# A graph layer's edge loop: the tiles that hold gathered table rows go from a ring of 6 to a ring of 12, placed in space that the unsorted records have left

## The chip, the cores and the metric

The kernel is one program on one core of a Trainium2 chip. Its time is the device time of one execution in microseconds (us). The kernel before was timed three times; the median counts. A separate profiled execution left the trace.

## The reference, cut to what matters

The layer has 1250 nodes of 512 features and 41250 edges, and then a feed-forward part with eight experts. Only the graph part touches the change:

```
xs = x[:, :C] @ W_in2f_s ; xv = einsum(x[:, C:], W_in2f_v)     # one table row of 4*128 values per node
sj = xs[idx_j] ; vj = xv[idx_j]                                # GATHER: one table row per edge
h  = shifted_softplus(f_ij @ Wf1 + bf1)                        # 20 radial values per edge -> 128
W  = (h @ Wf2 + bf2) * rcut_ij                                 # filter of each edge
s2, v2 = products of sj, vj and the edge's direction, times W
agg = segment_sum(x_ij, idx_i)                                 # sum over the edges of each target node
```

(Of the six parts of `W` the kernel needs four, since the last two feed nothing in the output.)

## The kernel before, in words

A first stage normalizes the nodes, builds the table `table_d` (1250 rows of 512 float32) in HBM, sorts the edges into 20 buckets by target node, and writes the edges' records back to HBM as `rec_d`. The unsorted records sit in the on-chip region `region_u` (10336 float32 per partition) until that write is over; after the edge loop the same region takes the transposed sums and then weights of the experts.

The edge loop (about 200 to 1256 us) goes through 342 tiles of 128 edges. Four tiles are a quad; three quads are one body of the hardware loop (12 tiles). What each engine does for tile t:

- GpSimd (POOL) issues two indirect DMAs, in one in-order queue. `gather_record(t + 6)` (L552) fetches 128 records of 32 values; it first waits until the product of the tile twelve before that record's tile is done (`prod_ready`), and its one-hots too. `gather_source(t)` (L563) fetches 128 table rows of 512 values by the indices in the record; it waits for the quad's records and, from t = 6 on, for `s_done`, the end of the summing matmuls of tile t - 6. Its target is `gath[:, t % 6]`. The POOL program is written out for all tiles, so its waits are on constants.
- TensorE (PE): per quad four `second_layer` matmuls (L1077, the filter W into a PSUM bank, ends `w_ready`), after the third of them `first_layer` of the next quad (L1068, ends `m1_done`), then four `sum_tile` (L1089 and L1096, which add the products into a bank by one-hots, end `s_done`). `sum_tile(t)` waits for `prod_ready` and for `flushed` of tile t - 3.
- VectorE (DVE): `products(t)` is two multiplications, L906 and L908; before them it waits for the rows (`rows_in`) and for `w_ready`. Between products stand `flush` (L920, adds a bank to the sums; one of a ring of three banks), `one_hot` (L897), `hidden` (L883) and `transpose_records` (L889, needs the records two quads ahead). In each quad the order is: product 0, flush of the quad before's tile 3, one-hot, products 1 to 3, flush 0, one-hot, hidden, flush 1, one-hot, transpose, flush 2, one-hot.
- ScalarE (ACT): scaled one-hots, the softplus (L669 waits for `m1_done`), and `seed`, which puts the constant part of W into a bank.
- SyncE's queue loads the residual input and the weights of one expert during the loop, each load after a given `prod_ready`.

After the loop come the node stage and the experts, which the change does not touch.

Of the kernel before, what the change touches and what calls it, by code (L numbers as in the profile page):

```python
# [15 lines left out]
P = 128  # L16
NODES, HID, FDIM, EDGES, RBF = 1250, 512, 128, 41250, 20
# [14 lines left out]
QUAD = 4  # L32
USED = (EDGES + BUCKETS * (P - 1)) // P
# [35 lines left out]
def tiles_of(left):  # L69

    return QUAD if left >= 1 else LAST
# [4 lines left out]


RING = 3
GRING = 6
PRING = 4  # L80
SRING = 3
SUM_BANKS = (0, 1, 7)
# [48 lines left out]
def hold(eng, semaphore, value, passed):  # L131

    eng.wait_ge(semaphore, value)
    eng.sem_inc(passed, 1)  # L134


def build(nc, x, src, rec_in, w_s, w_v, wf1, bf1, wf2, bf2, w1s, w1v, w2s, w2v,
          wg, wu, bu, wd, bd, out):
    ctx = ExitStack()
    with ctx:  # L140
        def sb(name, shape, dtype=F32):
            return ctx.enter_context(nc.sbuf_tensor(name, shape, dtype))

        def sem(name):
            return ctx.enter_context(nc.semaphore(name))


        table_d = nc.dram_tensor("table_d", [NODES, HID], F32, kind="Internal").ap()
# [4 lines left out]
        region_u = sb("region_u", [P, NCOLS * REC])  # L153
# [22 lines left out]
        slot_oh = region_r[:, at_slots:at_far].bitcast(BF16).rearrange("p (g s) -> p g s", g=OH_RING)  # L176
        far = region_r[:, at_far:at_far + FAR * P // 2].bitcast(BF16).rearrange("p (g s) -> p g s", g=FAR)

        gath = sb("gath", [P, GRING, HID])
        prod = sb("prod", [P, PRING, PRODS, FDIM])  # L180
        squares = prod[:, 2:4, :, :].rearrange("p a b c -> p (a b c)")[:, 0:4 * NCOLS].rearrange("p (k j) -> p k j", k=4)
        oneh = sb("oneh", [P, PRING, 4, WIDE])
# [75 lines left out]
        pool_passed = sem("pool_passed")  # L258
# [38 lines left out]
        recs_in = [sem(f"recs_in{r}") for r in range(RING)]  # L297
        rows_in = [sem(f"rows_in{g}") for g in range(GRING)]
        rec_t_ready = sem("rec_t_ready")
# [8 lines left out]
        prod_ready = sem("prod_ready")  # L308
        s_done = sem("s_done")
# [99 lines left out]
        with nc.Block() as block:  # L409
# [42 lines left out]
            def _(pool):  # L452
# [93 lines left out]
                def gather_record(t):  # L546

                    q, k = t // QUAD, t % QUAD
                    if q >= RING:
                        hold(pool, prod_ready, t - RING * QUAD + 1, pool_passed)  # L550
                        pool.wait_ge(ohy_ready, t - RING * QUAD + 1)
                    nc.gpsimd.indirect_dma_start(  # L552
                        out=recs[:, q % RING, k, :], out_offset=None, in_=rec_d,
                        in_offset=bass.IndirectOffsetOnAxis(ap=inv_i[:, t:t + 1], axis=0)).then_inc(recs_in[q % RING], 16)

                def gather_source(t):

                    q, k = t // QUAD, t % QUAD
                    if k == 0:
                        hold(pool, recs_in[q % RING], 16 * QUAD * (q // RING) + 16 * tiles_of(QUADS - 1 - q), pool_passed)  # L560
                    if t >= GRING:
                        hold(pool, s_done, 2 * (t - GRING + 1), pool_passed)
                    nc.gpsimd.indirect_dma_start(  # L563
                        out=gath[:, t % GRING, :], out_offset=None, in_=table_d,
                        in_offset=bass.IndirectOffsetOnAxis(
                            ap=recs[:, q % RING, k, R_DST:R_DST + 1].bitcast(I32), axis=0)).then_inc(rows_in[t % GRING], 16)

                pool.wait_ge(s_recd, 32)
                hold(pool, i_ready, 1, pool_passed)
                pool.wait_ge(s_wready, 2)  # L570
                for t in range(GRING):
                    gather_record(t)
                for t in range(USED):
                    if t + GRING < USED:
                        gather_record(t + GRING)
                    gather_source(t)

            @block.scalar
# [145 lines left out]
            def _(dve):  # L724
# [173 lines left out]
                                            rec[:, R_W:R_W + 1], ALU.is_equal, ALU.mult).then_inc(oh_ready, 1)  # L898

                def products(t, r, k, slot, body):  # L900
                    g, turn = (QUAD * r + k) % GRING, (QUAD * r + k) // GRING
                    s, v = gath[:, g, 0:FDIM], gath[:, g, FDIM:].rearrange("p (i f) -> p i f", i=3)
                    w = ps_w[slot].rearrange("p (k f) -> p k f", k=4)
                    dve.wait_ge(rows_in[g], body * 32 + 16 * turn + 16)
                    dve.wait_ge(w_ready, t + 1)
                    nc.vector.tensor_tensor(prod[:, slot, P_A:P_Q + 1:P_Q - P_A, :], w[:, W_A:W_Q + 1, :],  # L906
                                            s.unsqueeze(1).to_broadcast([P, 2, FDIM]), ALU.mult)
                    nc.vector.tensor_tensor(  # L908
                        prod[:, slot, :, :].rearrange("p (g k) f -> p g k f", g=2)[:, :, 1:4, :],
                        w[:, W_D:W_B + 1, :].unsqueeze(2).to_broadcast([P, 2, 3, FDIM]),  # L910
                        v.unsqueeze(1).to_broadcast([P, 2, 3, FDIM]), ALU.mult).then_inc(prod_ready, 1)
# [13 lines left out]
                def step(q, r, body, left=RING, first=False):  # L925

                    nxt, nbody, t = (r + 1) % RING, body + (r + 1) // RING, QUAD * q
                    here, then = tiles_of(left), tiles_of(left - 1)
                    products(t, r, 0, 0, body)
                    if not first:  # L930
                        flush_of(q - 1, (r - 1) % RING, 3)
                    if here == QUAD:
                        one_hot(t + 3, r, 3, 3, body, first=first)
                    for k in range(1, here):
                        products(t + k, r, k, k, body)
                    flush_of(q, r, 0, first=first)
                    if left >= 1:
                        one_hot(t + QUAD, nxt, 0, 0, nbody, n=then)
                        hidden(q + 1, nxt)
                    if here < QUAD:  # L940
                        return
                    flush_of(q, r, 1)
                    if left >= 1:
                        one_hot(t + QUAD + 1, nxt, 1, 1, nbody, n=then)
                    if left >= 2:
                        transpose_records((r + 2) % RING, body + (r + 2) // RING, n=tiles_of(left - 2))
                    flush_of(q, r, 2)
                    if left >= 1 and then == QUAD:
                        one_hot(t + QUAD + 2, nxt, 2, 2, nbody)
# [724 lines left out]
```

## Time and profile before

| what | us |
|---|---|
| median of 3 runs (1662.01 to 1665.01) | 1663.13 |
| the profiled execution | 1661.82 |
| its span, first to last instruction | 1660.1 |
| TensorE busy (matmuls) | 1366.3 (82%) |
| VectorE busy | 1068.0 (64%) |
| ScalarE busy | 826.0 (50%) |
| GpSimd busy | 797.8 (48%) |

"Busy" is time in instructions; waiting, branches and semaphore work do not count. In the groups by line, the part behind the bar is the idle time of the engine just ahead of these instructions, and what ended it. "remote" means that the wait ended at a semaphore's update for which the profile names no instruction; "issue" is idle time in which the engine waited for nothing that the profile shows.

### The profile page before, as it was taken

What the parts mean: (1) busy time and instruction counts of PE and PEld (TensorE: products, weight loads), DVE (VectorE), ACT (ScalarE), POOL (GpSimd) and SP (SyncE); (2) the same over time, 40 slices, a digit from 0 to 9 for tenths busy, and PEclk for the clock granted to TensorE, in tenths of its full rate; (3) what the DMA queues carried; (4) which work ended last, traced back from release to release, by engine and by line L of the source; (5) the groups of instructions that cost most, each with busy time, mean ns of one, the idle gap of its engine ahead of it and who ended that gap; (6) DMA issues with size and microseconds to landing.
All of it is one profiled execution on the core that took longest, in us unless ns stands there. A gap on an engine that the chain in (4) does not pass through costs nothing. (4 is left out here: it accounts for less than half of the span.)

```text
span 1660.1 us, 26803 instructions
## 1 busy us (share of the span) xinstructions
PE 1366.3 (82%) x7054; PEld 776.0 (47%) x7054; DVE 1068.0 (64%) x2530; ACT 826.0 (50%) x2145; POOL 797.8 (48%) x844
## 2 busy tenths in 40 slices
PE   0777688888888888888888888888899269999997
PEld 0552344444444444444444444444458146555554
DVE  6899567777777777777777777777787731111110
ACT  3679646556556556565565565565565201111111
POOL 2257556656656656666566566566550012222111
PEclk9999799999999999999999999999999569999999
DMA  5044133334333333333333333333342314554531
GB/s 218 1 191 128 37 88 91 104 99 106 103 86 106 94 96 105 107 104 111 104 100 94 88 88 94 87 91 91 87 106 89 130 57 142 168 179 144 148 81 20
DMA packets 65670, 172.66 MB, mean 104 GB/s; under 512 B 13963, under 2 KB 22523, under 8 KB 64989
## 3 DMA queue, kind: packets, MB, share of 16 engines
q0 software_dynamic: 43424, 105.53, 24.7%
q1 hardware_dynamic: 22196, 66.57, 11.2%
q8 instruction: 18, 0.29, 0.1%
q14 instruction: 32, 0.26, 0.1%
HBM read 148.72 MB, written 18.08 MB: 100 GB/s over the span
## 5 line engine op out<-in xcount | busy, mean ns | idle before, releaser
L1096 PE MATMUL PS<-prod,oneh 128*64 128x256 f32 x2052 | 508.4, 389 | 122.1 <-DVE region_s L920 87.2
L563 POOL DMA_INDIRECT gath<-table_d,recs x342 | 323.1, 945 | 307.1 <-PE PS L1089 211.8
L1096 PEld LDWEIGHTS PS<-prod,oneh 128*64 128x64 f32 x2052 | 259.7, 138 | 362.4 <-DVE prod L908 135.6
L1089 PE MATMUL PS<-prod,oneh 128*64 128x256 f32 x1368 | 375.7, 395 | 28.3 <-issue 26.9
L552 POOL DMA_INDIRECT recs<-rec_d,inv_i x342 | 323.1, 945 | 117.1 <-issue 116.5
L1077 PE MATMUL PS<-wf_sb,h_t 128*128 128x512 f32 x684 | 335.0, 613 | 2.9 <-issue 2.9
L908 DVE TENSOR_TENSOR prod<-PS,gath 128x768 f32<-128x768 f32 x342 | 324.1, 948 | 0.0
L684 ACT ACTIVATE oneh<-oneh,recs 128x64 f32<-128x64 f32 x1026 | 272.7, 336 | 77.6 <-issue 40.1
L906 DVE TENSOR_TENSOR prod<-PS,gath 128x256 f32<-128x256 f32 x342 | 143.8, 421 | 201.3 <-remote 152.5
L920 DVE TENSOR_TENSOR region_s<-region_s,PS 128x512 f32 x342 | 233.4, 683 | 44.3 <-issue 33.7
L669 ACT ACTIVATE soft<-PS,b1col 128x512 f32<-128x512 f32 x86 | 59.1, 687 | 322.0 <-remote 314.1
L691 ACT COPY PS<-c_rep 128x512 f32<-128x512 f32 x338 | 186.0, 581 | 43.2 <-DVE prod L908 22.1
L1089 PEld LDWEIGHTS PS<-prod,oneh 128*64 128x64 f32 x1368 | 155.9, 136 | 44.5 <-issue 40.2
L1077 PEld LDWEIGHTS PS<-wf_sb,h_t 128*128 128x128 f32 x684 | 118.6, 194 | 122.0 <-issue 122.0
L897 DVE TENSOR_SCALAR oneh<-iota_f,recs 128x64 f32<-128x64 f32 x342 | 106.0, 310 | 20.4 <-issue 10.1
L1487 ACT ACTIVATE region_s<-PS,bu_col 128x312 f32<-128x312 f32 x64 | 33.3, 520 | 164.3 <-PE PS L1602 164.3
L1068 PEld LDWEIGHTS PS<-rec_t,wf_sb 128*128 128x128 f32 x688 | 91.1, 193 | 46.6 <-issue 40.8
L1545 DVE TENSOR_TENSOR gath<-PS,region_x 128x512 f32<-128x512 f32 (+2 forms) x24 | 14.5, 603 | 139.1 <-PE PS L1617 115.7
L1452 POOL DMA_INDIRECT out<-gath,idx_add x24 | 40.2, 1677 | 128.9 <-ACT gath L1494 128.9
L1442 POOL DMA_INDIRECT region_x<-xn_d,idx_e x24 | 24.3, 1011 | 160.8 <-DVE idx_e L1519 155.1
L1068 PE MATMUL PS<-rec_t,wf_sb 128*128 128x128 f32 x688 | 91.7, 277 | 5.4 <-DVE rec_t L889 5.4
L1010 PE MATMUL PS<-region_r 128*128 128x344 bf16 x323 | 68.7, 314 | 27.5 <-ACT region_r L607 12.9
(270 smaller groups left out, 1481.8 us busy)
## 6 DMA issues: line engine op xcount, KB each, us to landing
region_r<-wu SPq DMA_DIRECT2D x16, 512.0 KB
region_r<-wd SPq DMA_DIRECT2D x16, 512.0 KB
region_u<-wu SPq DMA_DIRECT2D x16, 512.0 KB, 4.3
region_u<-wd SPq DMA_DIRECT2D x16, 512.0 KB, 5.4
recs<-rec_d,inv_i POOLq DMA_INDIRECT x342
gath<-table_d,recs POOLq DMA_INDIRECT x342
region_u<-rec_in SPq DMA_DIRECT2D x1, 5168.0 KB, 17.4
rec_d<-region_u SPq DMA_DIRECT2D x1, 5168.0 KB
```

What stands on the lines that cost most here:

```text
L552: nc.gpsimd.indirect_dma_start(out=recs[:, q % RING, k, :], out_offset=None, in_=rec_d, in_offset=bass.IndirectOffsetOnAxis(ap=inv_i[:, t: ...
L563: nc.gpsimd.indirect_dma_start(out=gath[:, t % GRING, :], out_offset=None, in_=table_d, in_offset=bass.IndirectOffsetOnAxis(ap=recs[:, q % ...
L684: last = nc.scalar.activation(oneh[:, slot, 1 + i, :], oneh[:, slot, 0, :], ACT.Copy, scale=recs[:, r, k, R_VEC + i:R_VEC + i + 1])
L691: nc.scalar.copy(ps_w[slot], c_rep[:, :]).then_inc(seeded, 1)
L897: nc.vector.tensor_scalar(oneh[:, slot, 0, :], iota_f[:, :], rec[:, R_LOCAL:R_LOCAL + 1], rec[:, R_W:R_W + 1], ALU.is_equal, ALU.mult).the ...
L906: nc.vector.tensor_tensor(prod[:, slot, P_A:P_Q + 1:P_Q - P_A, :], w[:, W_A:W_Q + 1, :], s.unsqueeze(1).to_broadcast([P, 2, FDIM]), ALU.mult)
L908: nc.vector.tensor_tensor(prod[:, slot, :, :].rearrange("p (g k) f -> p g k f", g=2)[:, :, 1:4, :], w[:, W_D:W_B + 1, :].unsqueeze(2).to_b ...
L920: nc.vector.tensor_tensor(block, block, PS[:, bank, :], ALU.add).then_inc(flushed, 1)
L1068: last = nc.tensor.matmul(to, wf1_sb[:, k, :], rec_t[:, r, :], start=k == 0, stop=k == QUAD - 1, skip_group_check=True)
L1077: nc.tensor.matmul(ps_w[slot], h_t[:, r, k * P:(k + 1) * P], wf2_sb[:, :, :].rearrange("p k f -> p (k f)"), start=False, stop=True, skip_g ...
L1089: return nc.tensor.matmul(PS[0:WIDE, bank, half * 2 * FDIM:(half + 1) * 2 * FDIM], oneh[:, slot, 0, :], prod[:, slot, 2 * half:2 * half + ...
L1096: return nc.tensor.matmul(to, oneh[:, slot, 1 + i, :], prod[:, slot, P_Q:P_B + i + 1:1 + i, :], start=i == 0, stop=i == 2, skip_group_chec ...
```

## The change

The ring of gathered rows has 12 tiles instead of 6 and lies at the start of `region_u`; `gath` keeps its 6 tiles for its other uses. Each of the 12 tiles has its own semaphore `rows_in`. A gather of rows waits from t = 12 on for the product of tile t - 12 instead of (from t = 6 on) for the sums of tile t - 6. The distance by which records run ahead of rows stays 6 and has a name of its own, `AHEAD`. In the vector program the tile and the awaited value follow from the place in the body alone.

```diff
-GRING = 6
+GRING = QUAD * RING
+AHEAD = 6
...
-        gath = sb("gath", [P, GRING, HID])
+        gath = sb("gath", [P, 6, HID])
+        rows = region_u[:, 0:GRING * HID].rearrange("p (g h) -> p g h", g=GRING)
...
                     if t >= GRING:
-                        hold(pool, s_done, 2 * (t - GRING + 1), pool_passed)
+                        hold(pool, prod_ready, t - GRING + 1, pool_passed)
                     nc.gpsimd.indirect_dma_start(
-                        out=gath[:, t % GRING, :], out_offset=None, in_=table_d,
+                        out=rows[:, t % GRING, :], out_offset=None, in_=table_d,
...
-                for t in range(GRING):
+                for t in range(AHEAD):
                     gather_record(t)
                 for t in range(USED):
-                    if t + GRING < USED:
-                        gather_record(t + GRING)
+                    if t + AHEAD < USED:
+                        gather_record(t + AHEAD)
                     gather_source(t)
...
-                    g, turn = (QUAD * r + k) % GRING, (QUAD * r + k) // GRING
-                    s, v = gath[:, g, 0:FDIM], gath[:, g, FDIM:].rearrange("p (i f) -> p i f", i=3)
+                    g = QUAD * r + k
+                    s, v = rows[:, g, 0:FDIM], rows[:, g, FDIM:].rearrange("p (i f) -> p i f", i=3)
                     w = ps_w[slot].rearrange("p (k f) -> p k f", k=4)
-                    dve.wait_ge(rows_in[g], body * 32 + 16 * turn + 16)
+                    dve.wait_ge(rows_in[g], 16 * body + 16)
```

## Rows read from the trace of the kernel before

**Rows 1.** The page's busy times: us, share of the span, instructions.

```profile
PE 1366.3 (82%) x7054; PEld 776.0 (47%) x7054; DVE 1068.0 (64%) x2530; ACT 826.0 (50%) x2145; POOL 797.8 (48%) x844
```

**Rows 2.** Groups by line and shape, loop only (204 to 1244 us): count, busy us, mean ns, idle before.

```profile
L1096 PE MATMUL PS<-prod,oneh 128*64 128x256 f32 x2017 | 500.5, 389 | 121.2 <-DVE region_s L920 87.2 <-DVE prod L908 16.3 <-issue 16.2
L563 POOL DMA_INDIRECT gath<-table_d,recs x338 | 319.4, 945 | 305.9 <-PE PS L1089 211.8 <-issue 54.3 <-PE PS L1096 34.4
...
L552 POOL DMA_INDIRECT recs<-rec_d,inv_i x331 | 312.4, 944 | 100.9 <-issue 100.5 <-ACT oneh L684 0.3
...
L906 DVE TENSOR_TENSOR prod<-PS,gath 128x256 f32<-128x256 f32 x335 | 140.9, 421 | 198.4 <-remote 152.5 <-PE PS L1077 38.3 <-issue 7.0
...
L889 DVE STREAM_TRANSPOSE rec_t<-recs 128x128 f32<-128x128 f32 x84 | 25.6, 305 | 0.0
```

**Rows 3.** Longest waits in the loop: us in total, times, longest us.

```profile
ACT soft L669 <- remote: 314.1, 82, 4.5
...
DVE prod L906 <- remote: 152.5, 88, 3.7
...
PE PS L1096 <- DVE region_s L920: 87.2, 83, 3.4
```

**Rows 4.** Windows: busy (count) of PE, PEld, DVE, ACT, POOL; clock; DMA share; GB/s.

```profile
260.00:507.70 247.70, 211.82 (x1119) 114.47 (x1119) 187.40 (x360) 143.55 (x380) 151.06 (x160) 0.99 0.37 100
507.70:755.40 247.70, 211.71 (x1124) 113.27 (x1122) 186.89 (x360) 143.63 (x380) 151.13 (x160) 1.00 0.36 101
755.40:1003.10 247.70, 211.43 (x1120) 113.10 (x1119) 187.26 (x360) 143.61 (x380) 151.05 (x160) 1.00 0.35 96
```

**Rows 5.** Row gathers (L563) begun before 508.5 us.

```profile
190.00:508.50 318.50, 96.39 (x102) 0.97 0.36 98
```

**Rows 6.** Products (L906) begun before 500.0 us.

```profile
190.00:500.00 310.00, 40.42 (x96) 0.96 0.36 97
```

**Rows 7.** Timeline of POOL: start, us, instruction, idle before.

```profile
505.05 0.94 POOL L552 DMA_INDIRECT recs<-rec_d,inv_i  x1 [0.30 <-issue]
508.73 0.94 POOL L563 DMA_INDIRECT gath<-table_d,recs  x1 [2.73 <-PE PS L1089]
```

**Rows 8.** Timeline of DVE from product 96 on, same columns.

```profile
500.40 0.42 DVE L906 TENSOR_TENSOR prod<-PS,gath 128x256 f32<-128x256 f32 x1
500.74 0.95 DVE L908 TENSOR_TENSOR prod<-PS,gath 128x768 f32<-128x768 f32 x1
502.06 0.69 DVE L920 TENSOR_TENSOR region_s<-region_s,PS 128x512 f32 x1 [0.37 <-issue]
503.51 0.32 DVE L897 TENSOR_SCALAR oneh<-iota_f,recs 128x64 f32<-128x64 f32 x1 [0.77 <-issue]
504.83 0.42 DVE L906 TENSOR_TENSOR prod<-PS,gath 128x256 f32<-128x256 f32 x1 [1.00 <-issue]
...
507.83 0.42 DVE L906 TENSOR_TENSOR prod<-PS,gath 128x256 f32<-128x256 f32 x1 [0.52 <-remote]
...
517.35 0.42 DVE L906 TENSOR_TENSOR prod<-PS,gath 128x256 f32<-128x256 f32 x1 [1.25 <-PE PS L1077]
...
520.28 0.42 DVE L906 TENSOR_TENSOR prod<-PS,gath 128x256 f32<-128x256 f32 x1 [1.64 <-remote]
```

**Rows 9.** Start of the loop: the third row gather, on POOL.

```profile
199.25 0.95 POOL L563 DMA_INDIRECT gath<-table_d,recs  x1 [0.30 <-issue]
```

**Rows 10.** Start of the loop: the third product, on DVE.

```profile
202.92 0.41 DVE L906 TENSOR_TENSOR prod<-PS,gath 128x256 f32<-128x256 f32 x1
```

**Rows 11.** Line L563: duration ns least/median/most, first and last start us.

```profile
L563 POOL DMA_INDIRECT gath<-table_d,recs x342: 940/946/958, 194.3 to 1241.5; - x171
```

**Rows 12.** Line L906, same columns.

```profile
L906 DVE TENSOR_TENSOR prod<-PS,gath x342: 410/419/427, 200.0 to 1252.3; 128x256 f32<-128x256 f32 x171
```

**Rows 13.** Line L908, same columns.

```profile
L908 DVE TENSOR_TENSOR prod<-PS,gath x342: 944/948/950, 200.4 to 1252.7; 128x768 f32<-128x768 f32 x171
```

**Rows 14.** Line L897, same columns.

```profile
L897 DVE TENSOR_SCALAR oneh<-iota_f,recs x342: 297/309/542, 191.7 to 1248.5; 128x64 f32<-128x64 f32 x171
```

## The prediction

> **What bounds the kernel now.** I read the busy times first, then the groups by line and the waits of the loop alone, then equal windows, and last the timeline around one tile, to see how early its rows are there.
>
> TensorE is busy for 1366.3 of 1660.1 us [rows 1], and 83 to 85% of the loop: 211.8 of 247.7 us in each of three windows [rows 4]. The three windows hold 160 POOL gathers each, so 80 tiles each: 247.7 / 80 = 3.10 us per tile, 12.39 per quad, with no window slower than another. The 342 tiles take some 1056 us at that pace, which is the stage in which the change can act.
>
> Who waits in it? POOL's row gathers stand idle for 305.9 us, of which 211.8 + 34.4 = 246.2 are ended by TensorE's summing matmuls (`s_done`) [rows 2]. This is the wait that the change takes away. It looks large, but POOL is no bound: two issues per tile take 2 x (0.945 + 0.30) = 2.49 of the 3.10 us. What matters is whether anybody waits for what POOL starts. Two instructions use it: the product (L906) and the transpose of records (L889). L889 has no idle time ahead of it at all in 84 executions [rows 2]. L906 has 198.4 us, 152.5 of them "remote", 88 times [rows 2, 3]. A product waits for two things, the rows and `w_ready`, so this has to be told apart.
>
> Tile 102 can be followed. 102 row gathers began before 508.5 us [rows 5], so the one at 508.73 is tile 102's [rows 7]. 96 products began before 500.0 [rows 6], so the one at 500.40 is tile 96's, 504.83 is 97's, 507.83 is 99's, and 517.35 and 520.28 are 102's and 103's [rows 8]. Tile 102's rows are thus asked for 517.35 - 508.73 = 8.62 us ahead of their product, and that product waited 1.25 us for the second layer on PE, by the profile's own naming. How long do rows need? At the start of the loop the third gather (tile 2) is issued at 199.25 and its product begins at 202.92 with no idle time before it [rows 9, 10]: rows are usable at most 3.67 us after the issue. Tile 102 has 8.62 - 3.67 = 4.95 us to spare. Tile 103's gather follows one record gather later, at about 508.73 + 2 x 1.24 = 511.2; its product at 520.28 is 9.1 us behind it, and yet it waits 1.64 us, "remote". So "remote" is not the rows: it is `w_ready`, and the same word stands before ScalarE's L669 (314.1 us, 82 times), which waits for `m1_done` of TensorE and for no transfer [rows 3]. Even in the loop's first tile the lead is 200.0 - 194.3 = 5.7 us and in its last 1252.3 - 1241.5 = 10.8 [rows 11, 12]. The loop goes round TensorE, the fourth product of a quad, flush 0 (87.2 us of TensorE's idle time end there, 83 times in 86 quads [rows 3]) and back to TensorE. Gathered rows are not in that circle.
>
> **The change, part by part.**
>
> The wait on `s_done` goes. 246.2 us of POOL's idle time lose their cause. On the path: 0, and the cover is the 4.95 us between the rows' landing and their product; only if that spare were below 0 would a microsecond of it count. What is late next for POOL: the record gather ahead of it in the queue. For tile 108's record it waits for product 96, which ends at 500.74 + 0.95 = 501.69 [rows 8]; the record gather then issues at about 501.99, and tile 102's rows at 501.99 + 0.94 + 0.30 = 503.2 instead of 508.73, some 5.5 us earlier. So the spare grows from 4.95 to about 10.4 us, unused. The lead does not become twelve tiles: records still run 6 ahead, and their own wait (product twelve back from tile t + 6, that is t - 6) now sets POOL's pace.
>
> The wait on the product twelve back comes. It is for an older product than the record gather just ahead of it has waited for, so it passes at once: 0 us. Queued behind it on POOL is the next record gather; for that one only the transposes wait, and they show no idle time. The number of waits is the same but for tiles 6 to 11, which lose theirs.
>
> Target and semaphores. The same 342 gathers of the same size land in another tile, 12 semaphores instead of 6. No row shows a landing in `region_u`; I take 0, since the DMA engines are at 0.35 to 0.37 of their time [rows 4], and each 0.01 us per landing would still be covered by the spare. Of the transfers moved earlier by 5.5 us, those that meet SyncE's weight and input loads merely meet them at another moment; windows with such loads (0.37 share) and with fewer (0.35) run at one pace [rows 4].
>
> DVE's wait before a product. One wait on the rows and one on `w_ready` as before; the awaited value has one term less. Below nothing it could give at most the 7.0 us of "issue" idle before L906 [rows 2]; above, a longer sequencer part costs nothing until it eats the idle time before the fourth product, and then up to 16 us (the rival below). I take 0, nearest to the row of a steady quad, where the products' idle time is ended by `w_ready`.
>
> A rule that speaks against the move: POOL's issues now come right behind the products and so stand beside other DVE work than before. The rows say that this has no price: line L563 took 940 to 958 ns in 342 issues, line L908 944 to 950, line L906 410 to 427 [rows 11 to 13], while POOL is busy 151 of 247.7 us [rows 4], so very many of them ran side by side. The Trainium skill, SBUF — State Buffer, section "SBUF: two separate sides", says that GpSimd cannot write a DMA's descriptors while VectorE holds the port pair that they share, in its two-port modes. If the one-hots did that, each issue would be late by an estimated 0.3 us at most, and by that the sum would still be 0, being far under the spare.
>
> **Sum.** 0 for the wait that goes, 0 for the one that comes, 0 for target and semaphores, 0 for DVE. The profiled execution would stay at 1661.8 (span 1660.1 plus 1.7 around it); the median of before is 1.3 us over it, so the forecast is **1663 us**. A difference can be told from none here from about 0.2%, 3.3 us, which is 39 ns in each of 86 quads.
>
> **The rivals.**
>
> A, faster: the rows do decide. If the 88 "remote" waits are rows, an issue 5.5 us earlier removes them, at most 152.5 us: 1663 - 152 = 1511; were only a quarter of them on the circle, 1625. For it speaks the size of POOL's wait and the word "remote". Against it: 4.95 us to spare at tile 102 and about 5.4 at tile 103, the 3.67 us at tile 2, and L669's like word. 3%.
>
> B, slower: the head of the loop's body on DVE. In the body's first quad DVE stands for 0.37, 0.77 and 1.00 us without a named cause (before the flush, the one-hot and product 97), and product 99 still has 0.52 us of idle time [rows 8]; that is the point from which it decides. If other register code for the twelve semaphores made each of the three products there 0.37 us later, the quad would lose 3 x 0.37 - 0.52 = 0.59 us, 27 bodies times 0.59 = 16 us: 1679. For it: these gaps exist and are on the engine whose code changes. Against: no wait is added. 7%.
>
> C, slower: DVE is held up by POOL's issues in their new place. If one DVE instruction per tile waited out an issue, 342 x 0.945 = 323 us: 1986. The one trace of it is L897's longest, 542 ns against a median of 309 [rows 14]; the durations of L906 and L908 speak against. 2%.
>
> D: the circle settles a little otherwise because semaphores and code stand elsewhere, without any of the above. It takes 39 ns per quad to leave the 0.2%; I give 10% to faster (about 1658) and 7% to slower (about 1668).
>
> E, that the change doesn't do what it says, is in part true and in the forecast: the wait named never decides, the record's does. It alters no time.
>
> **How the numbers follow.** Forecast 71%; faster 3 + 10 = 13%; slower 7 + 2 + 7 = 16%. The range for 8 in 10 runs from 1657.5 (D's faster side) to 1670 (D's slower side and the small end of B); A, C and most of B are left out.
>
> **What would show it.** POOL's L563 loses its idle time on PE L1089, and L552 gets some, ended by DVE L908; POOL's busy time stays near 797.8. Tile 102's gather comes some 14 us ahead of its product instead of 8.6. L906 keeps "remote" near 150 us, TensorE's L1096 keeps about 87 us on L920, and equal windows still hold 80 tiles in 247.7 us. A "remote" sum that falls by tens of microseconds would prove the rows (A) and me wrong; more "issue" before L906 and L897, with a longer first quad in each body, would be B; longer least and median durations on DVE would be C.

## The result, and the profile after

The changed kernel takes 1833.4 us (median of 4 runs, 1829.66 to 1833.92) against 1664.07 us for the kernel before (median of 4 runs, 1662.01 to 1668.94): a ratio of 1.1008, 95% interval 1.0979 to 1.1037. It is 10% slower, where no change was forecast. The profiled execution took 1833.81 us, its span 1832.1.

The page after, busy times and granted TensorE clock in 40 slices:

```profile
PE 1408.7 (77%) x7054; PEld 820.1 (45%) x7054; DVE 1045.5 (57%) x2530; ACT 831.3 (45%) x2145; POOL 797.6 (44%) x844
...
PEclk9899699898989998998999999898989958999999
```

Beside [rows 1] the counts are the same and POOL's busy time too (797.6 against 797.8 us). TensorE is busy 42.4 us more with the same 7054 matmuls, at a granted clock of 0.921 on the mean instead of 0.965. The span grew by 172.0 us, so most of it is waiting.

Groups by line of the whole execution (count, busy us, mean ns, idle before). Two lines more stand ahead of this code, so L1098 is L1096 of [rows 2], L565 is L563, L554 is L552, L908 is L906:

```profile
L1098 PE MATMUL PS<-prod,oneh 128*64 128x256 f32 x2052 | 553.7, 426 | 278.6 <-DVE prod L910 242.1
...
L554 POOL DMA_INDIRECT recs<-rec_d,inv_i x342 | 323.0, 944 | 470.3 <-DVE prod L910 378.4
...
L922 DVE TENSOR_TENSOR region_s<-region_s,PS 128x512 f32 x342 | 232.6, 680 | 392.6 <-remote 369.3
...
L565 POOL DMA_INDIRECT region_u<-table_d,recs x342 | 323.3, 945 | 109.3 <-issue 82.2
...
L910 DVE TENSOR_TENSOR prod<-PS,region_u 128x768 f32<-128x768 f32 x342 | 324.4, 948 | 0.0
...
L908 DVE TENSOR_TENSOR prod<-PS,region_u 128x256 f32<-128x256 f32 x342 | 142.8, 418 | 61.3 <-remote 39.8
```

The row gathers lost their idle time on TensorE, as forecast, and the record gathers got 378.4 us in its place, ended by the product. The product's "remote" fell from 152.5 to 39.8 us; a new one of 369.3 us stands before L922, DVE's flush. The durations of the gathers and products are the same as before.

Two windows, which answer to the three of [rows 4] (busy and count of PE, PEld, DVE, ACT, POOL; clock; DMA share; GB/s):

```profile
260.00:457.00 197.00, 152.99 (x781) 86.59 (x778) 125.22 (x249) 100.39 (x264) 105.31 (x112) 0.93 0.32 87
457.00:654.00 197.00, 151.65 (x784) 85.05 (x784) 124.89 (x249) 100.57 (x263) 105.79 (x112) 0.95 0.31 84
```

112 POOL gathers, so 56 tiles, in 197 us: 3.52 us per tile and 14.1 per quad, against 3.10 and 12.39 [rows 4]. The whole loop can be read from the line of the second product (duration least, median and most, first and last start):

```profile
L910 DVE TENSOR_TENSOR prod<-PS,region_u x342: 946/948/954, 202.1 to 1424.4; 128x768 f32<-128x768 f32 x171
```

From the first to the last of them it is 1222.3 us, where [rows 13] has 1252.7 - 200.4 = 1052.3. The loop holds 170.0 of the 172.0 us, at a mean of 14.3 us per quad.

The timeline of one quad after (start us, duration, instruction, idle before and what ended it): POOL, then TensorE, then DVE.

```profile
813.69 0.94 POOL L554 DMA_INDIRECT recs<-rec_d,inv_i  x1 [4.73 <-DVE prod L910]
814.94 0.95 POOL L565 DMA_INDIRECT region_u<-table_d,recs  x1 [0.31 <-issue]
816.19 0.95 POOL L554 DMA_INDIRECT recs<-rec_d,inv_i  x1 [0.30 <-issue]
...
821.20 0.95 POOL L554 DMA_INDIRECT recs<-rec_d,inv_i  x1 [0.30 <-issue]
822.45 0.95 POOL L565 DMA_INDIRECT region_u<-table_d,recs  x1 [0.30 <-issue]
...
818.95 0.59 PE L1098 MATMUL PS<-prod,oneh 128*64 128x256 f32 x2
819.47 2.84 PE L1079 MATMUL PS<-wf_sb,h_t 128*128 128x512 f32 x6
822.15 1.05 PE L1070 MATMUL PS<-rec_t,wf_sb 128*128 128x128 f32 x8
823.04 1.02 PE L1079 MATMUL PS<-wf_sb,h_t 128*128 128x512 f32 x2
...
811.96 0.95 DVE L910 TENSOR_TENSOR prod<-PS,region_u 128x768 f32<-128x768 f32 x1
...
816.37 0.95 DVE L910 TENSOR_TENSOR prod<-PS,region_u 128x768 f32<-128x768 f32 x1
...
825.20 0.69 DVE L922 TENSOR_TENSOR region_s<-region_s,PS 128x512 f32 x1 [5.36 <-remote]
825.80 0.31 DVE L899 TENSOR_SCALAR oneh<-iota_f,recs 128x64 f32<-128x64 f32 x1
826.03 0.42 DVE L908 TENSOR_TENSOR prod<-PS,region_u 128x256 f32<-128x256 f32 x1
```

POOL issues eight gathers in a row, with 0.30 us between, and then rests for over 4 us. TensorE has done the sums that L922 waits for by 818.95 + 0.59 = 819.54 at the latest, yet L922 starts at 825.20, in POOL's rest, 1.80 us after the last issue's end (822.45 + 0.95 = 823.40). The same place in the kernel before:

```profile
700.75 0.94 POOL L552 DMA_INDIRECT recs<-rec_d,inv_i  x1 [0.30 <-issue]
702.00 0.95 POOL L563 DMA_INDIRECT gath<-table_d,recs  x1 [0.30 <-issue]
703.25 0.94 POOL L552 DMA_INDIRECT recs<-rec_d,inv_i  x1 [0.30 <-issue]
706.85 0.94 POOL L563 DMA_INDIRECT gath<-table_d,recs  x1 [2.65 <-PE PS L1089]
...
699.75 1.05 PE L1068 MATMUL PS<-rec_t,wf_sb 128*128 128x128 f32 x8
...
705.92 0.69 ACT L669 ACTIVATE soft<-PS,b1col 128x512 f32<-128x512 f32 x1 [4.36 <-remote]
```

L669 waits for the first layer's matmuls (L1068), which end at 700.80. It starts at 705.92: 5.1 us later, and 1.73 us after the end of the issue at 703.25. That POOL's issues are the common term was read from the semaphore updates of the trace, over the quads of the loop:

```
                                        kernel before           changed kernel
last issue's end to TensorE's updates   1.74 us (1.68 to 1.80)  1.67 us (1.53 to 1.77)
POOL's rest per quad, median            2.70 us (85 rests)      4.69 us (83 rests)
```

(In brackets: 5 to 95%.) The update of L1068 itself comes 4.9 to 5.2 us after its matmuls' end in 76 of the 86 quads of before; outside the loop, TensorE's updates come 14 ns after an end in the same execution. In the loop the first ones of a row of issues still do: with POOL issuing since 813.69, the sums that end at 814.54 and 816.56 are reported 14 ns later. Then the updates fall behind, and most come in one burst some 1.7 us after the row's last issue, mostly 43 ns apart (in 36 of the 83 rests of the changed kernel a single one comes ahead of it). The table below takes three executions from 260 to 1000 us and counts how many of TensorE's updates came within 40 ns. In the changed kernel POOL issues eight gathers in a row, in s3 (below) four, and r3 is the same kernel as s3 in a session where nothing is late.

```
time since the first issue of the row    changed kernel   s3           r3
up to 3.75 us                            79 of 88         210 of 226   228 of 228
later, while POOL issues                 5 of 301         16 of 132    144 of 144
```

(Only updates of the first layer, the second layer and the second half of the sums; one that has no record counts as late.) In the kernel before, where a row starts sooner after the last burst, they fall behind earlier: 58 of 59 are on time in the first 1.25 us of a row, and 12 of 417 later. The recorded updates of VectorE and ScalarE in the same execution come on time.

With that the quad's length follows from POOL's issues and rests. Eight issues with their gaps take 8 x (0.945 + 0.30) = 8 x 1.245 = 9.96 us; to them comes the rest less one gap. Before: 9.96 + 2.70 - 0.30 = 12.36 us, where 12.39 was read. After: 9.96 + 4.69 - 0.30 = 14.35. POOL issues eight in a row in both kernels; the two rests differ in what ends them. The row gather of before waits for `s_done`, which is itself one of TensorE's held updates and comes with the burst: POOL goes on some 0.9 us later. The record gather of after waits for a product. In the quad shown, L922 starts 1.80 us after the last issue, the product 0.83 us behind it (after the one-hot), and it takes 1.28 us with its second half; in the quad before, POOL goes on 813.69 - (811.96 + 0.95) = 0.78 us after such a product. That makes 4.69. The quad is longer by 14.35 - 12.36 = 1.99 us, in 86 quads by 171 us. The spans differ by 172.0.

### The profile page after: what moved, and what is told of

Same layout as the page of the kernel before. It is cut to its first block and busy times, and to the rows that moved or that the text cites. A ratio compares the mean times of both kernels' runs of the same rounds, so it can differ in the third digit from the quotient of the medians.

```text
span 1832.1 us, 26771 instructions
## 1 busy us (share of the span) xinstructions
PE 1408.7 (77%) x7054; PEld 820.1 (45%) x7054; DVE 1045.5 (57%) x2530; ACT 831.3 (45%) x2145; POOL 797.6 (44%) x844
## 2 busy tenths in 40 slices
DMA packets 65670, 172.66 MB, mean 94 GB/s; under 512 B 13963, under 2 KB 22523, under 8 KB 64989
## 5 line engine op out<-in xcount | busy, mean ns | idle before, releaser
L1098 PE MATMUL PS<-prod,oneh 128*64 128x256 f32 x2052 | 553.7, 426 | 278.6 <-DVE prod L910 242.1
L1098 PEld LDWEIGHTS PS<-prod,oneh 128*64 128x64 f32 x2052 | 298.2, 153 | 523.5 <-issue 418.1
L554 POOL DMA_INDIRECT recs<-rec_d,inv_i x342 | 323.0, 944 | 470.3 <-DVE prod L910 378.4
L686 ACT ACTIVATE oneh<-oneh,recs 128x64 f32<-128x64 f32 x1026 | 282.1, 337 | 508.2 <-DVE oneh L899 459.3
L922 DVE TENSOR_TENSOR region_s<-region_s,PS 128x512 f32 x342 | 232.6, 680 | 392.6 <-remote 369.3
L1091 PE MATMUL PS<-prod,oneh 128*64 128x256 f32 x1368 | 428.9, 446 | 1.3 <-issue 1.3
L565 POOL DMA_INDIRECT region_u<-table_d,recs x342 | 323.3, 945 | 109.3 <-issue 82.2
L910 DVE TENSOR_TENSOR prod<-PS,region_u 128x768 f32<-128x768 f32 x342 | 324.4, 948 | 0.0
L908 DVE TENSOR_TENSOR prod<-PS,region_u 128x256 f32<-128x256 f32 x342 | 142.8, 418 | 61.3 <-remote 39.8
L1091 PEld LDWEIGHTS PS<-prod,oneh 128*64 128x64 f32 x1368 | 171.4, 153 | 9.2 <-issue 3.4
L899 DVE TENSOR_SCALAR oneh<-iota_f,recs 128x64 f32<-128x64 f32 x342 | 111.9, 328 | 4.9 <-DMA recs<-rec_d,inv_i 4.9
L1070 PEld LDWEIGHTS PS<-rec_t,wf_sb 128*128 128x128 f32 x688 | 91.0, 193 | 48.5 <-issue 42.4
L833 DVE TENSOR_SCALAR region_r<-iota_h,region_x 128x344 bf16<-128x344 f16 x323 | 89.8, 325 | 0.1
```

What stands on the lines that cost most here:

```text
L554: nc.gpsimd.indirect_dma_start(out=recs[:, q % RING, k, :], out_offset=None, in_=rec_d, in_offset=bass.IndirectOffsetOnAxis(ap=inv_i[:, t: ...
L565: nc.gpsimd.indirect_dma_start(out=rows[:, t % GRING, :], out_offset=None, in_=table_d, in_offset=bass.IndirectOffsetOnAxis(ap=recs[:, q % ...
L686: last = nc.scalar.activation(oneh[:, slot, 1 + i, :], oneh[:, slot, 0, :], ACT.Copy, scale=recs[:, r, k, R_VEC + i:R_VEC + i + 1])
L910: nc.vector.tensor_tensor(prod[:, slot, :, :].rearrange("p (g k) f -> p g k f", g=2)[:, :, 1:4, :], w[:, W_D:W_B + 1, :].unsqueeze(2).to_b ...
L922: nc.vector.tensor_tensor(block, block, PS[:, bank, :], ALU.add).then_inc(flushed, 1)
L1070: last = nc.tensor.matmul(to, wf1_sb[:, k, :], rec_t[:, r, :], start=k == 0, stop=k == QUAD - 1, skip_group_check=True)
```

## The experiments

The theory is that the wait does it, by moving and lengthening POOL's rest, while TensorE's updates are held by a long row of POOL's issues. Its rivals are the new place of the rows with its semaphores and code, and the rows' transfers themselves (bytes, landing writes, DMA engines).

One thing must be said of the sessions on the chips. The kernel before took 1662 to 1689 us in some (late sessions, below) and 1463 to 1466 us in others (clean sessions), on one and the same chip in one case. Each run is compared with the kernel before of its own session; a run of a clean session says nothing on the cause of the 10%. A result of one execution stands without an interval.

**e1: the new place, the old wait.** Late session.

```diff
-                    if t >= GRING:
-                        hold(pool, prod_ready, t - GRING + 1, pool_passed)
+                    if t >= AHEAD:
+                        hold(pool, s_done, 2 * (t - AHEAD + 1), pool_passed)
```

> The changed kernel with its ring of 12 tiles in region_u and its 12 semaphores, but a row gather waits for s_done of tile t - 6 again, as before the change. Theory P (pace: without the pause that s_done put into POOL's stream, TensorE's completions reach the other engines late): the loss goes, 1660 to 1668 us, quads of 12.4 us. Theory L (place: the landing in region_u, the 12 semaphores or the vector engine's other waits cost the time): it stays, 1825 to 1840 us, quads of 14.4 us.

Measured: 1670.35 us (10 runs) against 1665.72 (13 runs), ratio 1.002 (1.0002 to 1.0039).

**e2: the old place and ring, the wait on a product.** Late session; the edit is in the kernel before. With `GRING` still 6 the wait is for the product six tiles back, not twelve.

```diff
-                        hold(pool, s_done, 2 * (t - GRING + 1), pool_passed)
+                        hold(pool, prod_ready, t - GRING + 1, pool_passed)
```

> The kernel before with its ring of 6 tiles in gath, but a row gather waits for the product of tile t - 6 (enough for the ring to be safe) and not for its sums. Theory P: 1825 to 1840 us with everything else as before. Theory L: 1660 to 1668 us.

Measured: 1832.69 us (4 runs) against 1665.72, ratio 1.099 (1.0946 to 1.1034). The windows of e1 and then of e2:

```profile
260.00:457.00 197.00, 168.53 (x888) 91.63 (x886) 148.63 (x286) 114.95 (x304) 120.25 (x127) 0.98 0.37 100
```

```profile
260.00:457.00 197.00, 149.80 (x786) 84.02 (x782) 126.70 (x252) 101.06 (x266) 105.47 (x113) 0.96 0.32 87
```

127 gathers in 197 us with the old wait, 113 with the new. The two runs split the change: its target, its twelve semaphores and the other register code on DVE are worth 0.2% (0.4% at most), and giving up the wait on the sums is alone worth the whole 10%.

**e3: no row gathers** past tile 11 (the products read what the first twelve left there, so this kernel leaves out most of the gathering). Late session.

```diff
+                    if t >= GRING:
+                        return
                     nc.gpsimd.indirect_dma_start(
                         out=rows[:, t % GRING, :], ...
-                    dve.wait_ge(rows_in[g], 16 * body + 16)
+                    dve.wait_ge(rows_in[g], 16)
```

> The changed kernel without the row gathers after the first 12 tiles (products use old rows; the output is not the reference's in the sums); record gathers and their waits stay. If POOL's stream of gathers holds up TensorE's completions: the lag from the end of the first layer's matmuls to m1_done, about 5 us in both kernels, falls to under 1 us and quads take under 12.4 us (time under 1640). If the lag is TensorE's own (order of its work, half-array matmuls): lag and 14.4 us per quad stay, about 1830 us.

Measured: 1469.24 us against 1665.72. **e4: no gathers of records either** (past the first twelve tiles; the record gather returns too, and its waits are for the first landing alone).

> The changed kernel without row and record gathers after the first 12 tiles (12 tiles of records and rows are used over and over; the output is not the reference's in the sums). If gathers hold up TensorE's completions: lag at 14 ns as in the stages without gathers, quads at 10.5 to 11.5 us, time about 1520 to 1600. If it is TensorE's own: lag near 5 us, quads 12.4 or 14.4 us.

Measured: 1464.60 us, lower than the 1520 to 1600 expected. e3 and e4 are one execution each. The window of e3, and POOL's timeline in one of its quads:

```profile
260.00:457.00 197.00, 197.00 (x1122) 117.88 (x1121) 182.31 (x359) 144.45 (x380) 75.63 (x80) 1.00 0.09 19
```

```profile
399.75 0.95 POOL L554 DMA_INDIRECT recs<-rec_d,inv_i  x1 [4.39 <-DVE prod L912]
401.76 0.94 POOL L554 DMA_INDIRECT recs<-rec_d,inv_i  x1 [1.07 <-DVE prod L912]
403.01 0.94 POOL L554 DMA_INDIRECT recs<-rec_d,inv_i  x1 [0.30 <-issue]
404.26 0.95 POOL L554 DMA_INDIRECT recs<-rec_d,inv_i  x1 [0.30 <-issue]
410.18 0.95 POOL L554 DMA_INDIRECT recs<-rec_d,inv_i  x1 [4.97 <-DVE prod L912]
```

TensorE is busy for all of the window and the quad takes 9.85 us. POOL issues 80 gathers, one per tile, but not evenly: four in a row (with 1.07 us behind the first and 0.30 behind the next two), then a rest of 4 to 5 us. The hold-up is smaller here and not gone. The updates of sums that end behind the third issue come in a burst 0.87 us after the fourth has ended (median of 77 rests; 1.7 us after eight). The first and second layers end in POOL's rest or at the start of the next row, and their updates come after 14 ns, so nothing on TensorE's path is late. Taking the second half of the issues away, too, gives only 4.6 us more.

**e5: short rows.** The gather is kept with its indices but fetches 128 bytes per row from the records (so its products are of other data).

```diff
-                        out=rows[:, t % GRING, :], out_offset=None, in_=table_d,
+                        out=rows[:, t % GRING, 0:REC], out_offset=None, in_=rec_d,
```

> The changed kernel whose row gathers fetch 128 bytes per row (32 values of a record row) instead of 2048: the same 342 indirect DMAs with the same waits, a sixteenth of the bytes (products use mostly old data; the output is not the reference's in the sums). If the bytes in flight hold up TensorE's completions: as without row gathers, about 1470 us and 9.85 us per quad. If it is the indirect DMAs themselves, whatever their size: about 1830 us, 14.4 us per quad.

**e6: rows by SyncE.** POOL issues records alone; SyncE moves 128 whole rows of the table per tile (the same ones, so again other data) with a plain DMA of the full 256 KB. (The cut shows the rows alone; SyncE's loads of the input and weights keep their order in the same queue.)

```diff
 (SyncE, for each tile g)
+                    if g >= GRING:
+                        sp.wait_ge(prod_ready, g - GRING + 1)
+                    sp.dma_start(rows[:, g % GRING, :], table_d[0:P, :]).then_inc(rows_in[g % GRING], 16)
 (POOL, before the row gather)
+                    return
```

> The changed kernel whose rows come by plain DMAs of SyncE's queue (always the first 128 table rows, 256 KB each, so the output is not the reference's in the sums), each after the product of tile t - 12; POOL issues the record gathers alone. If transfers of this volume hold TensorE's completions up, from whatever queue: well above 1470 us, towards 1660 to 1830. If only POOL's gathers do: about 1470 us and 9.85 us per quad.

**e7 and e8: the wait on the sums four and eight tiles back**, in the new ring (e1's edit with 4 and with 8 for `AHEAD`).

> Ring of 12, a row gather waits for the sums of tile t - 4. With the pause theory, POOL's stream pauses once per quad as before; a longer hold-back gives TensorE's completions more gaps, so about 1665 us or less as long as rows still arrive in time; if rows arrive too late, products wait for them and the time rises over 1700 us.

> Ring of 12, a row gather waits for the sums of tile t - 8. With the pause theory this wait comes so early that the record gather's wait decides instead and the pause goes: about 1830 us. If any dependence on TensorE's sums is enough: about 1665 us.

Measured, all in a clean session with the kernel before at 1465.12 (one execution each, as in all runs from here on): e5 1462.23, e6 1450.18, e7 1529.73, e8 1465.82 us. None of the differences expected from the hold-up could appear, because the kernel before had none of it either: these four were inconclusive on the cause. They were run again, with the changed kernel itself:

> The changed kernel again, since the last four runs shared a chip on which the kernel before took 1465 us and no completion was late. If the lateness belongs to the chip: about 1833 us where the kernel before takes about 1664, and about 1465 us where the kernel before takes 1465. If it belongs to the kernel alone: about 1833 us on any chip.

> The same kernel as e5: row gathers of 128 bytes per row. On a chip where the kernel before takes about 1664 us: 1470 us if the bytes in flight hold TensorE's completions up, about 1830 us if the indirect DMAs themselves do. On a chip where it takes 1465 us it says nothing: 1462 us.

> The same kernel as e6: rows by plain DMAs of SyncE's queue. On a chip where the kernel before takes about 1664 us: 1450 us if only POOL's gathers of rows hold TensorE's completions up, 1660 to 1830 us if any transfer of that volume does. Elsewhere it says nothing: 1450 us.

> The same kernel as e8: a row gather waits for the sums of tile t - 8. On a chip where the kernel before takes about 1664 us: about 1830 us if the pause has to be long, about 1665 us if any wait for TensorE's sums is enough. Elsewhere 1465 us.

The session was clean again. r1 (the changed kernel) 1464.84, r2 (short rows) 1463.69, r3 (rows by SyncE) 1450.09, r4 (sums eight back) 1463.06, against 1463.21 us. The window of r1, and waits of it, columns as in [rows 3], the first from 260 to 654 us and the second from 204 to 1080:

```profile
260.00:457.00 197.00, 194.92 (x1095) 114.10 (x1092) 181.28 (x356) 143.51 (x375) 149.16 (x158) 1.00 0.45 125
```

```profile
ACT oneh L686 <- DVE oneh L899: 65.4, 149, 1.9
```

```profile
DVE prod L908 <- DMA region_u<-table_d,recs: 41.4, 60, 1.9
```

This is the same program as the one that took 1833 us. No "remote" is left among its long waits. POOL issues without a rest: 158 x 1.245 = 196.7 of 197 us, so here its issues are the bound, with TensorE 99% busy beside them, and now products do wait for rows, 60 times and 41.4 us in all. In a clean session the change makes no difference that one execution each could show (1464.84 against 1463.21, 0.1%).

**The third set** repeated the two sharpest, s1 in a clean session (1461.80 against 1465.77), s2 and s3 in a late one:

> The same kernel as e5 and r2 (row gathers of 128 bytes per row instead of 2048), to catch a chip on which TensorE's completions come late. Where the kernel before takes about 1664 us: about 1470 us if the bytes in flight hold the completions up, about 1830 us if the indirect DMAs themselves do, whatever their size. Where it takes 1465 us it says nothing.

> The same kernel as e5 (row gathers of 128 bytes per row), once more to catch a chip on which TensorE's completions come late. Where the kernel before takes about 1664 us: about 1470 us if the bytes in flight hold the completions up, about 1830 us if the indirect DMAs themselves do. Where it takes 1465 us it says nothing.

> The same kernel as e6 (rows by plain DMAs of SyncE's queue, 256 KB each). Where the kernel before takes about 1664 us: 1450 us if only POOL's gathers of rows hold the completions up, 1660 to 1830 us if any transfer of that volume does. Where it takes 1465 us it says nothing.

Measured: s2 1830.61 and s3 1451.62 us against 1662.37. The windows of s2 and then of s3:

```profile
260.00:457.00 197.00, 155.52 (x787) 87.12 (x788) 127.35 (x255) 101.88 (x268) 106.22 (x113) 0.93 0.08 17
```

```profile
260.00:457.00 197.00, 197.00 (x1123) 117.90 (x1121) 182.65 (x361) 144.93 (x380) 73.73 (x78) 1.00 0.45 126
```

VectorE's flushes waited for TensorE's sums in s3 and, in the clean session, in r3, the same kernel (204 to 1050 us):

```profile
DVE region_s L930 <- PE PS L1099: 27.7, 36, 1.3
DVE region_s L930 <- PE PS L1106: 19.2, 41, 1.1
```

```profile
DVE region_s L930 <- PE PS L1106: 1.3, 2, 1.1
```

s2 and s3 differ in the right way to tell bytes from issues. s2 moves 17 GB/s with two POOL issues per tile and is as slow as the changed kernel, its burst of updates coming 1.67 us after the last issue. s3 moves 126 GB/s with one POOL issue per tile (four in a row, then a rest, as in e3), in more DMA packets than the changed kernel (87558 against 65670 in the whole execution), and takes 1451.62 us against 1450.09 in the clean session. It has the small hold-up of e3 (0.87 us after the fourth issue; the waits above), which costs next to nothing. The load on the DMA engines, the landing writes and HBM are thus not what holds the updates; a long row of indirect DMAs from POOL is. Whether it is POOL's issuing or what its queue then does with these DMAs was not told apart, since each run that has fewer of the one has fewer of the other.

**t1 to t3: can the rest be given back?** If a rest of POOL lets the updates out, one placed well should cost less than it frees. t1 keeps the new wait and adds one in mid quad, on the second layer's `w_ready`:

```diff
+                    if t >= 9 and k == 1:
+                        hold(pool, w_ready, t - 1, pool_passed)
```

t2 and t3 are e8 and e7 again.

> Ring of 12; of every four row gathers the one of tile 4q + 1 waits for w_ready of tile 4q - 1 (the last second layer of the quad before), the others for the product twelve back alone. Theory H (on the chips in question TensorE's completions arrive only about 1.7 us after POOL's last issue, so POOL has to rest when the second layers end): where the kernel before takes about 1664 us, eight issues of 0.945 us, seven gaps of 0.30 and one rest of 1.7 give 11.4 us per quad instead of 12.4, about 1580 us. If the place of the rest does not matter: about 1664; if it takes the wait for sums: about 1830. Where the kernel before takes 1465 us: within 1% of that.

> The same kernel as e8 and r4 (a row gather waits for the sums of tile t - 8), for a chip where the kernel before takes about 1664 us. By theory H the wait leaves a rest in POOL's stream only if sums of tile t - 8 are still open when their gather's turn comes; with completions late that is so: between 1600 and 1700 us. If only the wait for t - 6 is long enough: about 1830.

> The same kernel as e7 (a row gather waits for the sums of tile t - 4), for a chip where the kernel before takes about 1664 us. If a longer rest of POOL brings TensorE's completions forward: under 1650 us. If rows then come too late, as they did where no completion is late (1530 against 1465): 1700 us or more. Where the kernel before takes 1465 us: 1530 again.

Measured: t1 1777.36 and t2 1838.44 us against 1688.24 (a late session, one execution each); t3 1529.86 against 1464.35 (a clean one). The waits of t1 from 260 to 654 us:

```profile
DVE region_s L924 <- remote: 124.6, 28, 7.0
...
POOL region_u L567 <- PE PS L1081: 59.5, 19, 3.8
```

t1 missed its expectation by far: 1580 was expected. The rest comes (3.3 us, median of 86), but at a moment at which both sums and second layers are open, so that it is again a wait for held updates and not beside them; in the session of these two, where t2 stands 150.2 us above the kernel before, it gives back 61.1 of them. t2 missed, too: 1600 to 1700 was expected if the wait for sums eight tiles back still made POOL rest. It did so before 12 of the 342 row gathers alone, and it is no faster than the product's wait. Of the waits tried in a late session the one for the sums six back, that of the kernel before, gives the shortest time. t3 came out as expected of a clean session and shows the other side: where nothing is held up, a nearer wait on the sums only costs, 65 us. Whether it gains in a late one is not known. No kernel that computes everything beat the kernel before.

## Why the prediction was wrong, point by point

**The step that failed** is the first: "The wait on `s_done` goes. 246.2 us of POOL's idle time lose their cause. On the path: 0", with the rows' 4.95 us as the cover. It counted only what POOL's gathers deliver. POOL's rest did something else: TensorE's held updates came out in it. Without the wait on `s_done` POOL rests until a product behind those updates has ended, for 4.69 us instead of 2.70: +171 us. That giving up the wait costs the 10% is shown by e2 (1.099), with e1 for all else (1.002). The mechanism was missing, and not a size wrong.

**The clue stood in the rows.** ScalarE's L669 had 314.1 us of "remote" [rows 3]. The text rightly took from it that "remote" is not the rows, and called it TensorE. It did not ask why L669 starts 5.1 us after the matmuls it waits for have ended, which the timeline of before shows. Had the end of L1068 been set beside the start of L669, the circle would have had a POOL term of 2.70 us per quad, and "POOL is no bound" would have been seen to be false: 8 x 1.245 + 2.70 - 0.30 gives 12.36 of the 12.39 us.

**A reading that was wrong.** The text lets tile 108's record gather issue at 501.99, right behind product 96, and gets rows 5.5 us earlier from it. But the row of that gather [rows 7] says 505.05, with 0.30 us of "issue" ahead of it, and the gather in front of it came without a wait, too:

```profile
503.80 0.95 POOL L563 DMA_INDIRECT gath<-table_d,recs  x1 [0.30 <-issue]
```

It came when POOL was through with the issues ahead of it, and no product held it. This was a second sign that POOL's issues set the pace.

**Right steps.** The record gather's wait on the product is what is late next for POOL (378.4 us on L554). The wait on the product twelve back itself nearly always passes at once (26.8 us ahead of 78 row gathers, most of them the usual 0.30). POOL's busy time stays (797.6). Target, semaphores and DVE's wait are nearly nothing (e1). The rows had time to spare: fetching 128 bytes instead of the whole row (s2) changes nothing, 1830.61 against the 1833.4 of the changed kernel in another late session. And where TensorE's updates are not held, the forecast "no difference" holds (r1), though there the rows have no time to spare.

**Wrong forecasts of the profile.** L906's "remote" was to stay near 150 us; it fell to 39.8, which the text would have taken for rival A, while the time rose. The sum had only gone to another consumer of the same burst: L669's and L906's became L922's. Of the 87.2 us on the flush 30.7 were left (37 times), and 242.1 us on the product came. Equal windows did not hold 80 tiles in 247.7 us but some 70.

**The rivals.** A (the rows decide) is excluded: the time rose, and s2, whose rows are a small part of the bytes, is as slow. e3's gain could be taken for the rows, but s3 moves them whole and has it too. B (the head of the body on DVE) is worth 4.6 of its 16 us (6.5 at the end of the interval): e1 has that code and is 0.2% up. C was the nearest in kind, POOL's issues in a new place that hold something up, at 2%; but it named DVE as the victim, whose durations are unchanged (948 and 418 ns), and its price of 323 us came from issues that DVE waits out. D (semaphores and code in another place) is what e1 tests: 4.6 us in 86 quads are 54 ns each, and not the 2 us that came. E was true as far as it went: the new wait never decides.

**The skill's rule** on descriptors and the port pair of VectorE and GpSimd (Trainium skill, SBUF — State Buffer, section "SBUF: two separate sides"), by which GpSimd cannot write descriptors while VectorE holds the pair in a two-port mode, had been weighed at 0. The gathers of after take 944 and 945 ns, as before, so no issue was lengthened and nothing of the loss is there; whether a one-hot of this kernel takes the pair at all, no run shows.

## What to carry to other kernels

An idle time that nobody seems to need can still be what lets others go on: before a wait is taken away, set the end of each producer beside the start of its consumer, and where they stand microseconds apart, find whose activity the gap follows. "Remote" names no transfer; here it was TensorE's updates behind POOL's issues. And compare a kernel with its neighbour in one session: what was worth 10% in one was worth nothing in the next.

## What the runs showed of the hardware

The way of the finding is told above; here its numbers stand together. In late sessions TensorE's semaphore updates fall behind while POOL issues indirect DMAs with 0.30 us between them. Those due early in a row of issues nearly all come on time: in the first 3.75 us in the changed kernel, e3 and s3, in the first 1.25 us in the kernel before. Later ones are held and come, mostly 43 ns apart, about 1.7 us after the end of the last of eight issues (1.67 in s2, 1.73 in e1, 1.74 in t1) and 0.87 us after the last of four (e3, s3). 128 bytes per row or the full row make no difference (s2); plain DMAs of SyncE at 126 GB/s add nothing (s3). VectorE's and ScalarE's updates are not held. In clean sessions the same programs show a lag of 14 ns, and the kernel before takes 1465 instead of 1664 us.

What sets the state, and by what way the updates are held, stays open: chip 7 was seen in both. The late traces have one more mark. Where POOL issues gathers, records of semaphore updates are missing for every engine: of VectorE's 1876, 1408 (the kernel before) to 1560 (the changed one) are there, and 1871 to 1876 in the clean runs and in e4, which has no gathers in the loop. So the recording may have a part in the hold-up. Each execution on record has a recorded span and clock, so no run shows what an unrecorded one would take. That the updates rather than the matmuls are late is read from the trace, and the late starts of L669 and L922 bear it out; that a long row of POOL's indirect DMAs causes it rests on taking half of them away (e3, s3), with the bytes kept or not.

A second effect was not tried by itself. In the loop of the changed kernel the granted clock is at 0.50, the level of 1.2 GHz, in 46 stretches, most of 3.4 us, 188 us in all, where the kernel before has 6 and 20 us. Ahead of each of the 46 TensorE had just stood idle for 1.7 to 3.9 us at a time. The windows after have 0.93 to 0.95 against 0.99 and 1.00 before [rows 4], and the summing matmuls of L1098 take 426 ns on the mean, those of L1096 389 [rows 2].
